# Moving an edge sort from layer 1 to the first blocks of layer 2, keeping eight count blocks, and spreading the weight additions anew

## What is computed

```
# GNN 1: A1 = number of edges from s to d (plus self loops), D1 = its degrees
h = relu(n1 * A1^T (n1 * (x @ W1)) + b1) ...           # four such convolutions, widths 128, 64, 128, 256
# FFN 1: the two best of 16 experts of each node, each a 256 -> 512 -> 256 MLP
# GNN 2: A2 = sum of edge weights from s to d
x = x + relu(n2 * A2^T (n2 * (layer_norm(x) @ W6^T)) + b6) ; the same with W7 ; x @ Wp^T + bp
# GNN 3: every edge adds a row of a table, chosen by its type and source, to its target
msgs = h_all[edge_types, src]; messages = segment_sum(msgs, dst) + bias
```

## Time and profile before

| | us |
|---|---|
| median of three runs | 4111.31 (4111.31, 4112.1, 4092.48) |
| the profiled execution | 4099.53 |
| its span on the core | 4097.8 |
| PE busy | 3047.5 (74%) |
| POOL busy | 2354.7 (57%) |
| DVE busy | 1745.2 (43%) |
| ACT busy | 1013.2 (25%) |
| granted TensorE clock, mean | 0.859 |
| chain that ended last, largest shares | PE 46%, POOL 14%, DVE 14% |

### The profile page before, as it was taken

How to read it: one execution, slowest core, us unless ns; L and a number is a source line. 1 busy time by engine, 2 the same in 40 slices (tenths; PEclk the granted TensorE clock), 3 DMA queues, 4 the chain that set the end, 5 groups by cost and what they waited for, 6 DMA issues and landing times.

```text
span 4097.8 us, 49188 instructions
## 1 busy us (share of the span) xinstructions
PE 3047.5 (74%) x16263; PEld 2194.5 (54%) x16264; DVE 1745.2 (43%) x4545; ACT 1013.2 (25%) x2147; POOL 2354.7 (57%) x1900
## 2 busy tenths in 40 slices
PE   4999976474587885887259999989997455555698
PEld 3555553353257655776248878865553233334465
DVE  6555535734366775101701112234443343444354
ACT  1666632212346541332400100012220000001121
POOL 5888888888776760677656656530002666662121
PEclk9999997777799995999679999989998566665799
DMA  6663232122456644778343443320215333335332
GB/s 246 177 195 66 5 37 1 0 18 2 123 134 182 143 110 124 203 212 210 38 120 127 143 133 120 130 76 31 71 61 167 90 95 91 90 94 128 106 121 76
DMA packets 284516, 440.11 MB, mean 107 GB/s; under 512 B 167039, under 2 KB 213523, under 8 KB 270565
## 3 DMA queue, kind: packets, MB, share of 16 engines
q1 hardware_dynamic: 118978, 285.09, 22.1%
q0 software_dynamic: 164448, 147.39, 18.5%
q10 hardware_dynamic: 864, 4.80, 0.3%
HBM read 318.97 MB, written 117.63 MB: 107 GB/s over the span
## 4 chain that ended last, share of the span: by engine, by line
PE 46%; POOL 14%; DVE 14%; issue 10%; DVEq 4%; DMA 4%; another core or an unknown queue 4%; ACT 2%; SPq 1%; ACTq 0%; POOLq 0%; PEldq 0%; PEld 0%
PE g_acc L2219 13%; POOL count_cells L483 9%; POOL weight_cells L1194 5%; PE f2m_pR L2900 4%; PE same_scores L1014 4%; DVE X L1281 3%; PE g3g_pp L1255 3%; PE f3e_pH L3230 3%; PE f2m_pR L2872 3%; PE f3e_pY L3239 2%; PE g_acc L1772 2%; PE same_scores L1018 1%; PE f2m_pO L2883 1%; DVEq L1281 1%
## 5 line engine op out<-in xcount | busy, mean ns | idle before, releaser
L1242 POOL DMA_INDIRECT g3g_got<-relations,g3g_idx x416 | 402.6, 968 | 612.5 <-ACTq L101 425.6
L1194 POOL DMA_INDIRECT weight_cells<-added_weight,added_row x391 | 632.2, 1617 | 211.3 <-issue 116.6
L483 POOL DMA_INDIRECT count_cells<-cells_count,added_row x391 | 649.5, 1661 | 154.1 <-issue 118.9
L2219 PE MATMUL g_acc<-g_H,g_blocks 125*125 125x256 f32 x2500 | 562.4, 382 | 56.7 <-DMA g_blocks<-weight_cells 44.3
L2219 PEld LDWEIGHTS g_acc<-g_H,g_blocks 125*125 125x125 f32 x2500 | 468.4, 189 | 132.2 <-issue 62.9
L1255 PE MATMUL g3g_pp<-g3g_got,g3g_hot 128*125 128x256 f32 x832 | 325.8, 540 | 285.6 <-issue 139.4
L2130 POOL DMA_INDIRECT slots_dram<-sort_rec,sort_row x392 | 380.5, 971 | 253.2 <-issue 117.8
L1255 PEld LDWEIGHTS g3g_pp<-g3g_got,g3g_hot 128*125 128x125 f32 x832 | 199.1, 262 | 412.8 <-issue 349.4
L1281 DVE TENSOR_TENSOR X<-X,g3g_pp 125x256 f32 x416 | 175.5, 422 | 355.0 <-issue 184.2
L1029 ACT ACTIVATE X<-same_scores 128x128 bf16<-128x128 f32 (+7 forms) x392 | 255.0, 651 | 171.8 <-PE same_scores L1018 135.4
L1843 ACT CAST g_blocks<-g_blocks 128x3125 f16<-128x3125 uint16 x85 | 235.8, 2795 | 91.6 <-DMA g_blocks<-count_cells 90.6
(11 more groups left out here) (728 smaller groups left out, 5533.2 us busy)
## 6 DMA issues: line engine op xcount, KB each, us to landing
g_blocks<-weight_cells SPq DMA_DIRECT2D x50, 1562.5 KB
g_blocks<-count_cells SPq DMA_DIRECT2D x85, 781.2 KB, 11.0
weight_cells<-edges_stripe POOLq DMA_DIRECT2D x25, 1562.5 KB
f1e_w<-in_L_ffn_w SPq DMA_DIRECT2D x68, 512.0 KB
relations<-f2m_ys SPq DMA_DIRECT2D x25, 896.0 KB
f_w<-in_L_ffn_w SPq DMA_DIRECT2D x16, 1024.0 KB
count_cells<-edges_XT POOLq DMA_DIRECT2D x19, 781.2 KB
f1e_b<-in_L_ffn_b SPq DMA_DIRECT2D x68, 128.0 KB
```

The costliest lines, as they stand in the source:

```text
L483: pool.indirect_dma_start(out=rows, out_offset=bass.IndirectOffsetOnAxis(ap=g.cell_row[:, t:t + 1], axis=0), in_=g.cell_count[:, t:t + 1], ...
L1194: pool.indirect_dma_start(out=rows, out_offset=bass.IndirectOffsetOnAxis(ap=g.cell_row[:, t:t + 1], axis=0), in_=g.cell_weight[:, t:t + 1] ...
L1242: pool.indirect_dma_start(out=got[:, j, :], out_offset=None, in_=table[:, :], in_offset=bass.IndirectOffsetOnAxis(ap=idx[:, n:n + 1], axis ...
L2219: last = nc.tensor.matmul(acc[0:P, i % 3, 0:D], blocks[0:P, i % BLOCKS, t * P:(t + 1) * P], H[p][0:P, t, :], start=(t == 0), stop=(t == T ...
```

## The change

`IN_PAUSE` becomes 1 and `BEFORE_EXPERTS` 264. A weight addition stands behind each of the 64 expert tiles. The weight additions are then 34 in the pauses, 230 in a row beside layer 1's GNN, 64 behind the tiles, and the same last 63 behind them. `RESIDENT` becomes 8: three blocks fewer are loaded and halved in each of passes 1 to 3, and 13 block loads are issued at the stage's start. The sort leaves layer 1 (with its loads on SP, its clears and steps on DVE, its two matmuls on PE, and the drain behind every block). In layer 2's GNN its loads stand on SP behind the weights and ahead of the first block load, its clears at the head of DVE's stream, its steps behind the takes of blocks 0 to 17, two at a time (the table `AT`), and PE's two matmuls behind block 3. Its buffers are arranged anew: `one` is a constant that is there already, `each` lies on `raw`.

```diff
-BEFORE_EXPERTS = 280
+BEFORE_EXPERTS = 264
...
-PAUSES, IN_PAUSE = 34, 2
+PAUSES, IN_PAUSE = 34, 1
...
-RESIDENT, STREAMED = 5, 5
+RESIDENT, STREAMED = 8, 5
...
-                if j == RESIDENT + STREAMED - 1:
-                    sort.load(sp, a)
...
-                        if p == 0 and j == sort.OFFSETS - 1:
-                            sort.sums_of_totals(pe)
...
-            sort.clear(dve)
...
-                    if j < T:
-                        sort.step(dve, p * T + j)
-                        dve.drain()
...
-    TOTALS, OFFSETS, RANKS, ROWS = 2, 13, [*range(14, 24), *range(75, 90)], 91
+    TOTALS, OFFSETS, RANKS, ROWS = 2, 7, range(8, 8 + T), 8 + T
+    SUMS = 3
+    AT = {0: (0, 1), 1: (2, 3), 2: (4, 5), 3: (6,), 4: (7, 8), **{k: (2 * k - 1, 2 * k) for k in range(5, 17)}, 17: (33,)}
...
+        self.one = self.g.ones[:, 0:ET]
+        self.each = self.raw[:, :, :].rearrange("p k e -> p (k e)").bitcast(BF16).rearrange("p (k e) -> p k e", k=6)
...
         gating.bank = ps("gate", [128, 512])
+        sort.rooms(ctx, gating.bank[:, 0:128].rearrange("p (k t) -> p k t", k=2))
...
+            sort.load(sp, a)
             for i in range(2 * T):
...
                         last.then_inc(summed, 1)
+                        if i == sort.SUMS:
+                            sort.sums_of_totals(pe)
...
         def _(dve):
+            sort.clear(dve)
             dve.wait_ge(w_loaded, 16 * 7)
...
                         dve.drain().then_inc(u_ready, 1)
+                        for k in sort.AT.get(i, ()):
+                            sort.step(dve, k)
+                            dve.drain()
...
-                    if n % 4:
-                        add_weight(nc, g, pool, BEFORE_EXPERTS + n // 4 * 3 + n % 4 - 1)
-
-            add_weights(nc, g, BEFORE_EXPERTS + SLOTS // 4 * 3, EC + 1)
+                    add_weight(nc, g, pool, BEFORE_EXPERTS + n)
+
+            add_weights(nc, g, BEFORE_EXPERTS + SLOTS, EC + 1)
```

More of the change, by code:

```diff
@@ L1669, with layer1_gnn @@
 EXPERT_LOADS = 4
-RESIDENT, STREAMED = 5, 5
-def layer1_gnn(nc, g, a, sort):
+RESIDENT, STREAMED = 8, 5
+def layer1_gnn(nc, g, a):
     WIDTH = (128, 64, 64, 128)
@@ L1717, in layer1_gnn @@
         psG, psU = shared[:, 0:3 * 128], shared[:, :].rearrange("p (k m) -> p k m", k=FOUR)
-        sort.rooms(ctx, shared[:, 3 * 128:512].rearrange("p (k t) -> p k t", k=2))
         loaded = [sem(f"loaded{k}") for k in range(RESIDENT + STREAMED)]
@@ L1993, in rooms @@
         self.raw = sb("raw", [128, 3, ET], I32)
-        self.key, self.pos, self.pad, self.tmp, self.hot, self.run, self.one = (
-            sb(m, [128, ET]) for m in ("key", "pos", "pad", "tmp", "hot", "run", "one"))
-        self.each = sb("each", [128, 5, ET], BF16)
+        self.key, self.pos, self.pad, self.tmp, self.hot, self.run = (
+            sb(m, [128, ET]) for m in ("key", "pos", "pad", "tmp", "hot", "run"))
+        self.one = self.g.ones[:, 0:ET]
+        self.each = self.raw[:, :, :].rearrange("p k e -> p (k e)").bitcast(BF16).rearrange("p (k e) -> p k e", k=6)
         self.tiles, self.padrow = sb("tiles", [1, ST]), sb("padrow", [128, 1])
@@ L2019, in clear @@
         nc.vector.memset(self.pos[:, :], 0.0)
-        nc.vector.memset(self.one[:, :], 1.0)
         nc.vector.memset(self.tiles[:, :], -1.0)
@@ L3360, in build @@
         g.out = out
-        sort.signals(keep)
-        layer1_gnn(nc, g, a, sort)
+        layer1_gnn(nc, g, a)
         kept.close()
@@ L3369, in build @@
         with ExitStack() as held:
+            sort.signals(held)
             loads = SharedExperts(nc, g, a, held)
```

## The result

The changed kernel took **4149.41 us** (median of four, 4141.90 to 4176.36), the kernel before 4107.02 in the same comparison (four runs, 4092.48 to 4112.10). The ratio is 1.0121, interval 1.0068 to 1.0174: slower, where I had forecast 4033 and 1.7% faster.

The account below looks back on a forecast made before the run. No engine was taken to bound the whole; PE carries under half the chain, POOL and DVE stand on it too. Terms -60 - 42 + 12 + 2 + 7 + 10 = -71 from 4103.9 gave 4033 us, range 4004 to 4082.

Parts of the forecast that it names:

- Pauses of layer 0: Layer 0's windows: fewer weight additions ahead of layer 1's start, -60 us (-61 to -57).
- Layer 1 without the sort: Layer 1: waits and longer block periods caused by the sort go away, -42 us (bounds 35 and 50).
- Does POOL follow?: POOL beside layer 1: about 30 us idle left ahead of the first gather, hiding the eighteen more additions.
- Expert tiles: Expert stage: a weight addition at all 64 tiles, most absorbed by POOL's waits, +12 us (+9 to +30).
- waits at the experts stay: Rival at the expert tiles: the 22 us of waits may be gather latency and remain, +18 us; chance 0.10.
- PE's wait behind block 3: Layer 2: PE waits for the counts behind DVE's take and a step, +7 us (bounds 6 and 10).
- The scatter comes late: Layer 2 and FFN 2: the last scatter lands at 827, delaying the table's copies, +10 us (0 to +48).
- both scatter rivals: Scatter slow while blocks load (4098 us, chance 0.08), or slow throughout (4217 us, chance 0.05).
- slow throughout: Rival: every scatter group takes 15.9 us behind large descriptors, a delay of 194 us, 4217 us; chance 0.05.

Follow-up runs that it names:

- e16: Changed kernel with five resident count blocks instead of eight; chip 15: 3948.32 us, 0.9864 of the kernel before.
- the first comparison: Unedited changed kernel against the kernel before, on a chip that isn't known: 4149.41 us against 4107.02, 1.0121.
- e6: Changed kernel with SP's wait for the scatters and the slots' reading back put behind the 20th table tile's stores; chip 14: 3923.36 us, 0.9814.
- e15: Changed kernel, unedited, on chip 15: 3949.79 us, 0.9866 of the kernel before.
- e11: Kernel before without the line in which a group of scatters waits for its block of layer 2; chip 1: 4221.81 us, 1.0293.
- e8: Kernel before without the scatters' wait for blocks of layer 2, on chip 14: 3989.00 us, 0.9983.
- e4: Changed kernel with each scatter group waiting for one more block of layer 2, counted from the 18th; chip 1: 4092.39 us, 0.9962.
- e12: e6 with scatter groups spaced by blocks, and from the 33rd group a landing wait after every two scatters; chip 1: 4018.65 us, 0.9810.
- e3: Changed kernel with only the first of 49 scatter groups sent, so layer 3 works on other slots; chip 1: 4088.08 us, 0.9965.

## Why the prediction was wrong

**Pauses of layer 0**: right in kind, -55 for -60. The landings are open by more than the 3 us that I gave them: 4.9 in three waits at the windows' starts where it had been 2.2, and 3.92 instead of 1.43 at the end. The 991 that I gave for layer 1's start was 60 less than 1051, the time of POOL's first read of the counts (1051.01); that read stands at 995.85 now, within the 1000 that I had set. PE's first matmul of the layer, 9 us behind it, moved from 1060.0 to 1005.0, and lies between 999 and 1013 in the other runs with the new pauses.

**Layer 1 without the sort**: right, -44 for -42. That the resident blocks count for nothing was right (e16).

**Does POOL follow?** Half right. POOL had 6.64 us left ahead of the gather, not 30. It still hid the additions, with hardly any margin.

**Expert tiles**: the term was mis-sized: +24 for +12, with +2 for the rest of the way, which measured under 1. It lies within its bounds of 9 and 30. I had argued that POOL would absorb most of its waits; from the first gather to the 64th tile the stage took 320.0 us for 296.3, and 24 of the 30 that 16 x 1.90 makes stayed. The rival "waits at the experts stay" (+18 more) was nearer than my own value.

**PE's wait behind block 3**: right. 19.7 us lie between the starts of blocks 3 and 4, 11.9 between undisturbed ones: +7.8 for +7.

**The scatter comes late**: its clock was right to a few us and its consequence was not. It started 230.5 us behind layer 2's first matmul (232 forecast), and SP's reading back, which waits for the last landing, was issued 828.2 behind it (landing forecast at 827). But the step went on: "The delay is 827 + 1 + 6 - 824 = **+10**". The 824, the time at which the sixth table tile asks, was taken from the kernel before, as though layer 2 and FFN 2 would run at their old pace beside a scatter in a new rhythm. In the first comparison they ran 54 and 73 us slower, and the table was too late to wait at all. On chip 15 they ran faster, the table asked earlier, and the wait was 24.07 us; e6 (chip 14) removes it with SP's later read and needs 289.4 us from first to last table copy where e15 needs 315.1.

**The step that failed** is the one that isn't there: what the scatter does to the others. The sum had layer 2's 50 blocks at +7 and the way to the table at 0, and they measured +54 and +73. In both scatter rivals I asked whether transfers slow the scatter. The rival on the slower side, "slow throughout", died by its own sign (a group took 12.2 us on average, with single ones of 15, not 15.9), and the time was lost all the same. I had the rows to ask. The diff left `pool.wait_ge(multiplied, c // AT_ONCE)` as it was while the count that it compares with no longer started at zero; a wait that the change makes empty is a part of the change. And four blocks of the kernel before took 14 to 18 us for 10.6 with "issue" and "remote" as what they waited for: 634.4 - 610.3 = 24 us of the same hold-up, if the undisturbed chip's blocks are the measure. Where the hold-up is missing the forecast comes near: on chip 15 the ratio is 0.9866 where 4033 / 4103.9 is 0.983, 52 us less than before where I had 71. The kernel before has no profile on a chip without the hold-up, so the gap can only be estimated from the first comparison's terms: the experts' 10 and the table wait's 14 beyond mine make 24, where 19 are missing. Nothing in my sum stood for the scatter's neighbours, nor for the chip.

**What stays open.** Why the chips differ: no row of the trace tells. What inside the core delays matmuls whose data are there and takes whose releaser is done: the trace shows the delay ("issue", "remote") and not its cause. It has a rhythm, though. PE's weight loads in e11's disturbed stretch:

```profile
2360.28 0.28 PEld L2218 LDWEIGHTS g_acc<-g_H,g_blocks 125*125 125x125 f32 x1 [0.45 <-issue]
2360.99 0.29 PEld L2218 LDWEIGHTS g_acc<-g_H,g_blocks 125*125 125x125 f32 x1 [0.43 <-issue]
2361.71 0.28 PEld L2218 LDWEIGHTS g_acc<-g_H,g_blocks 125*125 125x125 f32 x1 [0.43 <-issue]
```

They start 0.71 us apart, and in the 120 us around them steps of 0.7 and of 1.4 us come again and again, where e8 has 0.22 nearly throughout. So it looks as if they waited for turns at something, and what it is isn't shown. All runs here carry a profile, so whether recording takes part in it isn't known. How much of the closeness is itself a result is open too: in e11 groups 15 to 28 follow each other at 11.2 to 11.5 us just while blocks 16 to 19 take 20 to 46 us, and with block loads held up, a landing has nothing beside it. The edits of e4, e11 and e12 show which way the cause runs, not how much of e11's 138 us in the blocks feeds itself. Whether a slower rate alone, without a tie to the blocks, ends it while layer 2 runs was tried only on chips without it; for FFN 2, e12's pairs on chip 1 say yes.

## What to carry to other kernels

A wait against a running count is an order of work; when its step is moved, work out afresh at which value the count stands when it starts. Ask of each stream of small transfers both what slows it and what it slows, and look in the trace of before for blocks that are longer than their neighbours with "issue" or "remote" beside them. And measure a change of one or two per cent on more than one chip before calling it a gain or a loss: this one was both, and only the version that keeps the scatters apart (e12) was clearly ahead on the chip where it mattered. Then compare a fast and a slow chip stage by stage: most of the difference lay in layer 3, which the change never touched.

## What the runs showed of the hardware

Indirect stores issued by POOL can hold back engines with which they share no data. On chip 1 and in the first comparison, groups of eight stores (128 rows each) at 11.2 us with 1.4 us of landing between them cut PE from 558 matmuls in 120 us (e8) to 191 (e11), made DVE start about 19 us behind its releaser, and cost the changed kernel 145 and 156 us in 733 (878.0 and 888.8, against e3's 733.2). At about 12.5 us per group (one per block) the cost was near 20 (e12 639.1, e4 639.0, e3 619.6), and in pairs at 15.3 us none on the way to the table (112.0, e3 113.6). Beside indirect gathers at 1.25 us each, layer 3 and what follows took 952 to 958 us on chip 1 and 879 to 882 on chips 8, 14 and 15. The Trainium skill's page "SBUF — State Buffer", in "SBUF: two separate sides", has the DMA side and the engines' side of the memory unable to contend, and PE never waiting on anyone there. On chips 8, 14 and 15 the runs agree: PE is busy for 607.79 of 611 us beside 387 scatters. On chip 1 PE is busy for 79.15 of 120 us beside 80 scatters. No run tells whether the memory's ports have a part in that, so the page's rule isn't refuted; taken as a promise that POOL's transfers can't slow PE, it fails there, and the measurement decides.

The chips differ by as much as the changes do: the same kernel before took 4001 to 4006 us on chips 8, 14 and 15 and 4099 to 4106 on chip 1.
